# One decoder layer: TensorE's projection and first scores are moved ahead of the global queries' turn

## The reference

```python
# x (16, 256, 128), ctx (16, 64, 96); 16 heads of 8
def attn(x):                       # stage "self"
    mask = same block of 64 | key is one of 8 global tokens | query is one of 8 global tokens
    q, k, v = split_heads(x @ Wq + bq), split_heads(x @ Wk + bk), split_heads(x @ Wv + bv)
    scores = where(mask, q @ k.T / sqrt(8), -inf)
    return (softmax(scores) @ v).merge_heads() @ Wo + bo
x = x + attn(layernorm(x))
x = x + mlp(cross_attention(layernorm(x), ctx))          # stage "cross"
x = x + top2_of_16_experts(layernorm(x)) + shared_expert(layernorm(x))
```

## Time and profile before

| what | us |
|---|---|
| median of 3 runs | 567.05 |
| lowest and highest | 566.04, 572.32 |
| profiled execution | 568.54 |
| its span in the trace | 566.7 |

### The profile page before, as it was taken

One profiled execution on the slowest core, in us unless ns is written; L12 is line 12 of the kernel. 1 busy time (PEld: TensorE's weight loads), 2 busy tenths in 40 slices (PEclk: granted clock), 3 DMA queues, 4 the chain that ended last, 5 costly groups with the idle time before them and its releaser, 6 DMA issues. The chain is left out here.

```text
span 566.7 us, 17496 instructions
## 1 busy us (share of the span) xinstructions
PE 469.9 (83%) x6139; PEld 348.1 (61%) x6139; DVE 409.6 (72%) x1247; ACT 296.8 (52%) x757; POOL 298.4 (53%) x588
## 2 busy tenths in 40 slices
PE   1977888888888888888999999999767999999810
PEld 1755666666666666545676676666544888888610
DVE  7566999999888888876889898987572434434337
ACT  2573665555556656524656656564424444444237
POOL 5543454444444334201358888777771577777720
PEclk9997999999999999969999999999989999999975
DMA  6626343455655655326233333332124334333158
GB/s 189 112 51 139 55 71 63 67 132 111 110 108 110 108 107 114 81 52 150 54 83 90 95 87 97 96 85 67 34 97 132 106 110 116 110 109 98 53 178 286
DMA packets 96006, 58.30 MB, mean 103 GB/s; under 512 B 24560, under 2 KB 92224, under 8 KB 95920
## 3 DMA queue, kind: packets, MB, share of 16 engines
q1 hardware_dynamic: 74448, 39.93, 30.2%
q10 hardware_dynamic: 16896, 7.34, 6.7%
q0 software_dynamic: 4576, 9.91, 5.1%
HBM read 20.76 MB, written 17.50 MB: 68 GB/s over the span
## 5 line engine op out<-in xcount | busy, mean ns | idle before, releaser
L507 POOL TENSOR_SCALAR veps<-mv 128x2 f32<-128x2 f32 x48 | 11.2, 232 | 144.9 <-issue 101.2
L1292 ACT ACTIVATE probs<-ps 128x512 f32<-128x512 f32 x128 | 73.3, 603 | 12.1 <-PE ps L1672 9.8
L613 POOL DMA_INDIRECT expert_in<-xn,sloti x64 | 65.5, 1023 | 17.6 <-issue 17.6
L1147 DVE TENSOR_TENSOR eh<-ps,sg 128x256 f32<-128x256 f32 x40 | 17.0, 425 | 59.8 <-ACT sg L1496 58.9
L772 DVE TENSOR_REDUCE nmax<-ps 128x8 f32<-128x512 f32 x64 | 42.5, 686 | 18.9 <-PE ps L1607 18.8
L666 POOL DMA_INDIRECT expert_out<-ey,xt x40 | 38.3, 957 | 27.0 <-DVE ey L1154 16.7
L772 DVE TENSOR_REDUCE mparts<-ps 128x8 bf16<-128x512 f32 x64 | 43.3, 687 | 6.7 <-PE ps L1662 6.3
L1607 PE MATMUL ps<-kbd,qs 96*64 96x128 bf16 x512 | 38.0, 293 | 4.5 <-DMA qs<-part 3.6
L2026 PE MATMUL ps<-wgu,turned 128*128 x160 | 41.3, 380 | 0.0
L1490 ACT COPY turned<-ps 128x512 f32<-128x512 f32 (+1 forms) x43 | 23.8, 554 | 28.5 <-PE ps L2019 23.2
L509 POOL TENSOR_TENSOR rstd<-veps,minus_half 128x2 f32<-128x2 f32 x48 | 35.8, 745 | 4.0
(11 more groups left out here) (248 smaller groups left out, 1360.2 us busy)
## 6 DMA issues: line engine op xcount, KB each, us to landing
kbd<-part SPq DMA_DIRECT2D x192, 32.0 KB
qs<-part ACTq DMA_DIRECT2D x93, 64.0 KB
xt<-expert_in SPq DMA_DIRECT2D x64, 72.0 KB
qs<-part SPq DMA_DIRECT2D x51, 64.0 KB
ck_scr<-wgu SPq DMA_DIRECT2D x6, 512.0 KB
ckbd<-ck_scr SPq DMA_DIRECT2D x16, 192.0 KB
kbd<-part SPq DMA_DIRECT2D x48, 64.0 KB
wgu<-in_L_ffn_gate_up_w SPq DMA_DIRECT2D x4, 512.0 KB, 4.0
```

Of the source, the lines that this page charges most:

```text
L613: pool.indirect_dma_start(xs, bass.IndirectOffsetOnAxis(sloti[b % 3][:, n:n + 1], 0), xn3[b % 3][:, n // TOPK, n % TOPK, :], None).then_in ...
L1292: a_.activation(probs[:, 2 * i:2 * i + 2, :], P2[i % 2][:, :].rearrange("p (j q) -> p j q", j=2), ACT.Exp, scale=SCALE).then_inc(s("probs" ...
```

## The change

For bodies 0 to 13 (`late(b)`):

- TensorE: behind `global_keys(b)` come the projection of b+2 and the first score group of b+1, and only then the turn of the global queries of b. The other score groups alternate with the values of the global keys and the product of the global queries. The output product of b-1, which stood right behind `global_keys`, comes behind the four score groups; since the projection of b+2 now lies in the same bank, it waits for ScalarE's two copies of it (`qk32`).
- VectorE: the maximum of the global queries comes right behind the transpose inside `attended`, the reciprocal of their sum behind `global_rows`; the first row maximum of b+1 ahead of normalising; the rest for the second part behind the third row maximum; the residual addition of b-1 behind the last one.
- TensorE's wait for the residual addition (`x_new`) moves from the projection to the transposes of the next body.
- POOL's counter `kbg` is merged into `kgqg`, with the counts changed to match (`headed`).

ScalarE's order and the transfers are not changed. Bodies 14 to 16 keep the old order on TensorE and VectorE, apart from the early maximum and reciprocal.

```diff
+        def late(b):
+            return 0 <= b < B - 2
+        def headed(b):
+            return 3 * b + 2
...
-            def attended(b):
+            def attended(b, between):
...
                 v.transpose(turned_od, OD[:, :]).then_inc(s_("od_turned"), 1)
+                between()
                 dve.wait_ge(s_("od_turned"), b + 1)
...
                 if has(b - 1):
-                    attended(b - 1)
-                if b == 0:
+                    attended(b - 1, lambda: global_query_max(b) if has(b) else None)
+                elif has(b):
                     self_last_part(1)
-                if has(b):
                     global_query_max(b)
                 if has(b - 1):
                     global_rows(b - 1)
+                if has(b):
+                    global_query_sum(b)
                 if has(b + 3):
                     stats(s_, b + 3, self_arrived)
...
-                if has(b):
-                    global_query_sum(b)
-                if has(b - 1):
+                if has(b - 1) and not late(b):
                     self_end(b - 1)
...
+                if late(b):
+                    self_maxima(b + 1, 0, 0)
                 if has(b + 3):
                     normalise(s_, b + 3)
...
-                self_maxima(b + 1, 0, 0)
+                if not late(b):
+                    self_maxima(b + 1, 0, 0)
                 self_maxima(b + 1, 0, 1)
-                if has(b + 2):
+                if not late(b):
+                    if CROSS and b + 2 == B:
+                        cross_rest(0)
+                    if has(b):
+                        global_heads_out(b)
+                self_maxima(b + 1, 1, 0)
+                if late(b):
                     self_rest(b + 2, p)
-                elif CROSS and b + 2 == B:
-                    cross_rest(0)
-                if has(b):
                     global_heads_out(b)
-                self_maxima(b + 1, 1, 0)
                 self_maxima(b + 1, 1, 1)
                 if has(b + 1):
                     whole_max(b + 1)
                     self_vg(b + 1, 1 - p)
-                    if has(b + 2):
+                    if late(b):
+                        if has(b - 1):
+                            self_end(b - 1)
                         self_last_part(b + 2)
...
             def self_project(b):
                 pe.wait_ge(s_("xnT"), b + 1)
-                at_least(pe, s_("x_new"), b - 2)
...
             def self_out(b):
                 pe.wait_ge(s_("att_all"), b + 1)
+                if late(b + 1):
+                    pe.wait_ge(s_("qk32"), 2 * (b + 3) + 2)
...
                 if has(b + 1):
                     self_global_scores(b + 1, 1 - p)
+                at_least(pe, s_("x_new"), b - 1)
                 if has(b + 2):
                     columns(s_, b + 2, 2)
...
                 if has(b):
                     global_keys(b, p)
-                if has(b - 1):
-                    self_out(b - 1)
-                if has(b):
+                if late(b):
+                    self_project(b + 2)
+                    self_scores(b + 1, 1 - p, 0, 0)
                     global_query_turn(b)
-                if has(b + 2):
-                    self_project(b + 2)
-                elif CROSS and b + 2 < B + 2:
-                    pe.wait_ge(s_("x_new"), b)
-                    cross_project(b + 2 - B)
-                if has(b + 1):
-                    self_scores(b + 1, 1 - p, 0, 0)
+                    self_scores(b + 1, 1 - p, 0, 1)
                     self_global_values(b + 1)
-                    self_scores(b + 1, 1 - p, 0, 1)
-                if has(b):
+                    self_scores(b + 1, 1 - p, 1, 0)
                     global_query_out(b, p)
-                if has(b + 1):
-                    self_scores(b + 1, 1 - p, 1, 0)
                     self_scores(b + 1, 1 - p, 1, 1)
+                    if has(b - 1):
+                        self_out(b - 1)
+                else:
...
```

More of the change, by code:

```diff
@@ L554, in self_global_keys @@
                                          kbd[p][0:KROWS, :, :, :, :].rearrange("p j a k n -> p j a (k n)")[:, :, :, first:first + step * (n - 1) + 1:step])
-                last.then_inc(s_("kbg"), 1)
+                last.then_inc(s_("kgqg"), 1)
             def lay_out_later_stages(b):
-                pool.wait_ge(s_("kgqg"), 2 * b + 4)
+                pool.wait_ge(s_("kgqg"), headed(b + 1))
                 for p in range(2):
@@ L1248, in self_first_part @@
                 act.wait_ge(s_("qk_ps"), 2 * b + 2)
-                at_least(act, s_("kgqg"), 2 * b - 2)
+                at_least(act, s_("kgqg"), headed(b - 2))
                 a_.activation(qk[p][:, 0:S], A0[:, 0:S], ACT.Identity, bias=cols[:, 0:1]).then_inc(s_("qk32"), 1)
@@ L1612, in self_global_scores @@
             def self_global_scores(b, p):
-                pe.wait_ge(s_("kgqg"), 2 * b + 2)
+                pe.wait_ge(s_("kgqg"), headed(b))
                 at_least(pe, s_("probs"), 4 * (b - 1))
@@ L1701, in global_keys @@
                 pe.wait_ge(s_("probs"), 4 * b + 3)
-                pe.wait_ge(s_("kbg"), b + 1)
+                pe.wait_ge(s_("kgqg"), headed(b) + 1)
                 for odd in range(2):
@@ L1756, in self_body @@
                     weigh(s_, b, p, 0, lambda n, j: vbd[p][:, n, j, :], NB)
-                if has(b - 1):
-                    if has(b + 2):
-                        pe.wait_ge(s_("xnT"), b + 3)
-                    elif CROSS and b + 2 < B + 2:
+                if has(b - 1) and not late(b):
+                    if CROSS and b + 2 < B + 2:
                         pe.wait_ge(c_("xnT"), b + 3 - B)
@@ L1771, in self_body @@
                     global_keys(b, p)
-                if has(b - 1):
-                    self_out(b - 1)
-                if has(b):
+                if late(b):
+                    self_project(b + 2)
+                    self_scores(b + 1, 1 - p, 0, 0)
                     global_query_turn(b)
-                if has(b + 2):
-                    self_project(b + 2)
-                elif CROSS and b + 2 < B + 2:
-                    pe.wait_ge(s_("x_new"), b)
-                    cross_project(b + 2 - B)
-                if has(b + 1):
-                    self_scores(b + 1, 1 - p, 0, 0)
+                    self_scores(b + 1, 1 - p, 0, 1)
                     self_global_values(b + 1)
-                    self_scores(b + 1, 1 - p, 0, 1)
-                if has(b):
+                    self_scores(b + 1, 1 - p, 1, 0)
                     global_query_out(b, p)
-                if has(b + 1):
-                    self_scores(b + 1, 1 - p, 1, 0)
                     self_scores(b + 1, 1 - p, 1, 1)
+                    if has(b - 1):
+                        self_out(b - 1)
+                else:
+                    if has(b - 1):
+                        self_out(b - 1)
+                    if has(b):
+                        global_query_turn(b)
+                    if CROSS and b + 2 < B + 2:
+                        pe.wait_ge(s_("x_new"), b)
+                        cross_project(b + 2 - B)
+                    if has(b + 1):
+                        self_scores(b + 1, 1 - p, 0, 0)
+                        self_global_values(b + 1)
+                        self_scores(b + 1, 1 - p, 0, 1)
+                    if has(b):
+                        global_query_out(b, p)
+                    if has(b + 1):
+                        self_scores(b + 1, 1 - p, 1, 0)
+                        self_scores(b + 1, 1 - p, 1, 1)
                 if CROSS and b + 1 == B:
```

## The result

The kernel after took 587.68 us (median of 6 runs, 584.22 to 590.57), the one before 569.23 beside it (6 runs): a ratio of 1.0329, 95% interval 1.0285 to 1.0374. **Slower by 3.3%**, 18.5 us, where 583 us and a loss of 15.6 were predicted. Its profiled run took 588.07 us with a span of 586.2; the span of before was 566.7, so 19.5 us are to be found.

A forecast was written before the change was run, and what follows sets the result against it. No engine full; a chain through several, with transfers arriving last in half the bodies, set the body. The closed loop, 2.7 + 11.4 = 14.1 us in 14 turns, adds 15.6: 584.1, less 1.5 for the median, 583 us; range 568 to 595.

The forecast's parts named there:

- The loop: Self stage: transfers landed, first scores, query turn, pgqT copy, cast, transfers again; claimed 14.1 us a turn, 13.0 now.
- 2.72 us from scores to cast: Loop's part from L to the next cast: scores 0.56, query turn 0.44, engine hop 0.06, pgqT to cast 1.66.
- D: Self stage: time from the start of ScalarE's cast to L, the deciding term, taken as 11.4 us.
- the other half: The seven of fourteen bodies whose transfers arrived before they were asked for; D there between 10.2 and 11.7, middle 10.9.
- The low end, 10.2: Lower end of D, from the slice where DMA work ends and from the skill page's fixed cost of 2.0 us.
- the light body: Body with its cast at 45.34 and little other traffic; its DMA work ends ten and a fifth us later.
- The sum: 14 turns of 14.1 us from 45.30 put body 15's scores at 242.7; loss 15.6 us, carried to the end.
- The clock, taken as 0: TensorE idling 2.8 us a body may halve its clock; 0 in the sum, up to 6.2 us in the range.
- the 6.2 allowed: Upper price of the clock: the query turn 0.44 us longer at half speed, in 14 turns.
- TensorE ready 2.8 us before L: TensorE's own work in a body is 11.3 us, so it is ready some 2.8 us before L.
- L: The moment in a body when all eighteen transfers into kbd and qs, awaited by the next scores, have landed.
- The terms at nothing: Output product behind the scores and VectorE's new order: no stall or up to 0.5 us, covered by 2.8 us.

The follow-up runs named there:

- dose: Kernel after plus one more ScalarE activation (about 0.48 us, result unread) ahead of the two the cast needs, in sequences 2 to 15: 591.21 us, ratio 1.0399.
- the change of neighbours: Kernel before with SP's zeroed expert rows, context-key scratch writes and expert-weight loads put behind the landing of the key transfers: 567.9 us, ratio 0.9995.
- the kernel with the projection back: Kernel after with TensorE's order query turn, projection, first scores; output product and VectorE's order stay those of after: 574.65 us, ratio 1.0093.

## Why the prediction was right, and where its sizes were off

**The loop** was the step that decided, and it holds. It is seen in the trace of after (scores, turn, copy, cast, transfers, scores), opened by moving the turn back or the cast forward, and its bodies lengthened by a dose. Filling TensorE doesn't shorten it.

**2.72 us from scores to cast** was measured as 2.70 in 9 of 14 bodies and 2.78 on the mean; the others came 0.1 to 0.3 later, two with ScalarE still at copies of the same body, three with the query turn at half speed (0.69 us).

**D, taken as 11.4**: from cast to the next scores 11.56 on the mean of 13 bodies (the 14th, below), from 11.0 to 12.1. That 11.4 came so near is in part luck. Of the seven waits of the earlier trace rows three are the 0.33 us that the weight load of the scores idles in bodies without such a wait too; the three readings of D are the highest of the seven, which have a mean of 11.77 and not 12.0; and 10.9, put in for the other half, was too low. The two errors nearly cancel. The low end, 10.2 as in the light body, did not come. The Trainium skill's fixed cost of about 2.0 us ("DMA: Bandwidth & Descriptors", Anatomy of one DMA) is given there for transfers that GpSimd issues; GpSimd's two, whose issue the profile times to the landing, took 3.9 us here (median of 28).

**The sum** had 242.7 for the scores of body 15; they came at 246.69, 4.0 later. By its terms: the start 0.6 earlier; 14 x 0.06 = 0.8 for the cast; 13 x 0.16 = 2.0 for D; 1.5 for the last body (cast 233.83, scores 246.69: 12.86); 0.3 is 14.12 rounded to 14.1.

**The clock, taken as 0,** is the mis-sized term in that last body: from 233.0 to 239.8 it was at half speed (window above), TensorE came late, and its scores row has no wait for a transfer, alone among those shown. Other runs bear this out: where the last body kept full clock, D is 11.5 to 11.6 in it (with TensorE filled, with the dose, with the other transfers behind the landing); where it lost it, 12.86 again (the two transfers on GpSimd). The windows of that body in the last two of these, columns as above:

```profile
227.13:241.43 14.30, 12.31 (x174) 8.63 (x175) 11.90 (x34) 8.61 (x23) 6.03 (x18) 1.00 0.55 99
...
230.02:245.58 15.56, 14.44 (x174) 10.30 (x175) 11.08 (x32) 8.01 (x21) 6.24 (x19) 0.78 0.62 126
```

So the clock cost about 1.4 us there and 0.25 in each of the three bodies with a slow turn, out of the 6.2 allowed. The Trainium skill ("TensorE: Matmul & The Clock Gate", HAM oscillation) says that a loop which waits for DMA each turn loses the clock each turn; the trace agrees in most bodies, 0.908 against 0.961 on the whole, but three of the fourteen kept 0.97 to 1.00, and here the waits that stood ahead of the half-speed stretches also hid most of their price.

**TensorE ready 2.8 us before L** was too much: its eleven waits on kbd are 1.4 us on the mean (15.6 in all), because half-speed stretches and waits for VectorE's maxima (3.0 us in 6) took part of it. The forecast needed only that something was left.

**The terms at nothing** (output product behind the scores, VectorE's order) are not seen inside the loop, as said: the kernel that leaves them out and has the turn behind the scores (only the query turn moved, 588 us) is no faster, though another chain ends its bodies. They aren't free in themselves: with the loop open and the projection back in its place they cost 0.9% (0.6 to 1.2).

So the change splits, by the ratios: +0.9% for the output product and VectorE's order, +0.9% for the projection ahead of the turn, +1.4% for the scores ahead of the turn. The first and the last are clear of noise, the second is not sure, as said above. And the split holds in this order only: from the kernel before, with its output product and VectorE's order, the turn behind projection and scores cost 3.8% by itself. For the second there is this explanation, which is worked out and not shown: a turn's cast and landing take 2.45 + 11.4 = 13.85 us, and first scores to next turn 11.5 to 11.8, so two bodies can't be shorter than 25.4 to 25.7 us, 12.7 to 12.8 each; the kernel before has bodies of 12.8 and is at that bound already. It would also fit that the early maximum and the change of neighbours gave nothing, though for the maximum the waits above name the output product. The first is read from the trace and wasn't tested by itself: ScalarE's waits for the reciprocal (3.2 us in 11), and two bodies of 14.8 us at half clock.

No version beat the kernel before; the best of them equal it.

## What to carry to other kernels

Before a step is moved past a wait for transfers, follow what stands behind it on every engine down to the cast or copy that feeds those transfers: if the walk comes back to the wait, the body is at least as long as that ring, and the ring is a sum of a few rows. A wait of half a microsecond in a chain may be what gives the transfers their time; taking one out bought nothing here, because the next waits in line took its place. A delay of a known size put into a suspected ring, sized by the pitch at which it delays the next instruction and read body by body rather than from the total, tells whether the ring is the bound.

## What the runs showed of the hardware

In the kernel after, waits on kbd of 1.3 to 2.8 us opened eight bodies, and all eight had a stretch at half clock (granted 0.76 to 0.88); 0.80, 0.28 and 0.22 us opened bodies at 1.00, 0.97 and 1.00, and two bodies without a wait had 0.88 and 0.89. The length of the wait does not settle it: 1.80 us opened a body at 1.00 with the other transfers behind the landing, and waits of 1.6 us on the mean ahead of the turn (21.0 in 13) came with half clock in only two bodies of the kernel with the projection back. 0.73 and 0.54 us, parted by a product, left it at 1.00 in both windows of before. Two activations of 256 columns, 0.48 us each, follow each other at 0.36. And taking two of twelve issues off SP, 1.26 us of its time in the body shown, moved the landing by 0.07 there and by 0.15 on the mean.
